# Who adds and who multiplies: moving GpSimd's share in the scan stages of a decoder layer

## What is computed

```
def step(h, inputs):
    d_t, B_t, C_t, u_t = inputs
    dA = jnp.exp(d_t[..., None] * A)
    h = h * dA + (d_t * u_t)[..., None] * B_t[:, None, :]
    y = jnp.einsum('bdn,bn->bd', h, C_t)
    return (h, y)
...
y = jnp.swapaxes(ys, 0, 1) + u * D
y = y * jax.nn.silu(jnp.transpose(z, (0, 2, 1)))
return jnp.einsum('md,bld->blm', out_proj_weight, y)
```

## Time and profile before

| | |
|---|---|
| median of 3 runs | 1690.67 us (1690.46 to 1693.57) |
| the profiled execution | 1690.69 us, its span 1688.9 us |
| PE busy | 1438.1 us, 85% |
| DVE busy | 1341.3 us, 79% |
| POOL busy | 1059.8 us, 63% |
| ACT busy | 798.7 us, 47% |
| chain that ended last | PE 55%, DVE 17%, issue 12%, ACT 8%, POOL 7% |

### The profile page before, as it was taken

The page is one execution under the profiler, slowest core; times in us unless marked ns, Lnnn a source line. Parts: engine busy times, 40 slices in busy tenths (PEclk is TensorE's granted clock), DMA queues, the critical chain, the costliest instruction groups (busy, mean ns, idle before and its releaser), DMA issues.

```text
span 1688.9 us, 19487 instructions
## 1 busy us (share of the span) xinstructions
PE 1438.1 (85%) x5448; PEld 834.8 (49%) x5456; DVE 1341.3 (79%) x2215; ACT 798.7 (47%) x1370; POOL 1059.8 (63%) x684
## 2 busy tenths in 40 slices
PE   7587669999699899999699899999699999737994
PEld 4333224444565565444465565444465665326783
DVE  3588999676799999786899999796899999784212
ACT  3676444246634565246634565246634565231141
POOL 0299899102999899402999899401999999422101
PEclk9889899999699999999699999999699999967997
DMA  3550000413535673613535674612534773600984
GB/s 114 224 187 25 1 0 23 146 32 109 198 137 182 205 236 126 212 38 105 227 118 188 208 235 138 212 38 101 231 113 163 226 235 124 249 25 20 349 331 142
DMA packets 94074, 252.14 MB, mean 149 GB/s; under 512 B 11024, under 2 KB 11152, under 8 KB 88848
## 3 DMA queue, kind: packets, MB, share of 16 engines
q1 hardware_dynamic: 86688, 229.93, 40.1%
q0 software_dynamic: 5120, 16.78, 3.1%
q10 hardware_dynamic: 2160, 4.19, 0.6%
HBM read 207.87 MB, written 42.99 MB: 149 GB/s over the span
## 4 chain that ended last, share of the span: by engine, by line
PE 55%; DVE 17%; issue 12%; ACT 8%; POOL 7%; DMA 1%; DVEq 0%; POOLq 0%; SPq 0%; ACTq 0%
PE bank L1936 11%; PE bank L1796 7%; DVE bank L1269 5%; PE bank L2062 5%; PE bank L1809 5%; PE bank L1868 4%; PE bank L1873 4%; POOL work L662 3%; PE bank L1965 3%; PE bank L1957 3%; PE bank L1862 3%; DVE work L1281 2%; PE bank L1912 2%; DVE pairs L1281 2%; PE bank L1837 2%
## 5 line engine op out<-in xcount | busy, mean ns | idle before, releaser
L662 POOL TENSOR_TENSOR work<-du,BB 128x1024 f32<-128x1024 f32 x255 | 598.7, 2357 | 5.2 <-DVE work L1545 4.4
L941 ACT ACTIVATE bank<-delta,A_sb 128x512 f32<-128x512 f32 x512 | 350.0, 690 | 471.9 <-DVE pairs L1281 257.8
L1269 DVE TENSOR_TENSOR_SCAN bank<-bank,work 128x512 f32<-128x512 f32 x432 | 522.6, 1219 | 7.8 <-POOL work L662 4.0
L1936 PEld LDWEIGHTS bank<-x3T,ew_up 128*128 128x128 f32 x1488 | 220.7, 196 | 74.3 <-issue 63.2
L1936 PE MATMUL bank<-x3T,ew_up 128*128 128x128 f32 (+1 forms) x1488 | 242.8, 310 | 5.2 <-issue 5.2
L1281 DVE TENSOR_TENSOR pairs<-bank,CB 128x512 f32<-128x512 f32 x240 | 161.6, 673 | 3.9 <-PE bank L1873 2.9
L607 POOL TENSOR_TENSOR col<-col,halfpow 128x4 f32<-128x4 f32 (+1 forms) x8 | 7.8, 973 | 208.1 <-DVE col L1421 208.1
L1281 DVE TENSOR_TENSOR work<-bank,CB 128x512 f32<-128x512 f32 x192 | 128.7, 670 | 0.0
L1809 PE MATMUL bank<-xT,wst 128*128 128x512 f32 x256 | 120.2, 616 | 9.1 <-DVE ew_up L1258 7.0
L1868 PE MATMUL bank<-pairs,ident 128*128 128x512 f32 x160 | 87.5, 630 | 41.8 <-POOL pairs L717 16.7
L2062 PE MATMUL bank<-wst,zg 128*128 128x512 f32 x256 | 117.0, 593 | 0.9 <-DVE zg L1289 0.9
(11 more groups left out here) (256 smaller groups left out, 2511.8 us busy)
## 6 DMA issues: line engine op xcount, KB each, us to landing
ew_up<-in_exp_w SPq DMA_DIRECT2D x93, 512.0 KB, 3.7
ew_dn<-in_exp_w SPq DMA_DIRECT2D x93, 256.0 KB, 4.3
hm<-xs_dram SPq DMA_DIRECT2D x69, 256.0 KB, 4.6
ys_dram<-x3T SPq DMA_DIRECT2D x69, 256.0 KB, 4.6
wst<-in_w_in SPq DMA_DIRECT2D x64, 256.0 KB, 2.7
BB<-bc_dram SPq DMA_DIRECT2D x16, 1024.0 KB, 7.4
CB<-bc_dram SPq DMA_DIRECT2D x16, 1024.0 KB, 9.4
wst<-in_out_w SPq DMA_DIRECT2D x32, 256.0 KB, 2.9
```

What stands on the lines that cost most here:

```text
L662: nc.gpsimd.tensor_tensor(dBu[:, k % CHUNK_SLOTS, :, :], du[:, j % 2:j % 2 + 1, :].broadcast_to([P, 2, T]), BB[:, n0:n0 + 2, :], ALU.mult) ...
L941: nc.scalar.activation(R[q % RING][:, :], delta[:, j, :], ACT.Exp, scale=A_sb[:, j, n:n + 1]).then_inc(S["da_ready"], 1)
L1269: V.tensor_tensor_scan(prod[c % (2 * PAIR_SLOTS)] if on_pool(q) else R[q % RING][:, :], R[q % RING][:, :], dBu[:, c // 2 % CHUNK_SLOTS, c ...
L1936: ins = mm(gu_bank(v)[:, part * n:(part + 1) * n], w[:, part * D + k * P:part * D + (k + 1) * P], rhs, start=(k == 0), stop=(k == KD - 1))
```

## The change

Two rules change, with all that counts by them. `on_pool` is now true for every fourth unit (3, 7, 11, ...) in all batches; in batch 0 it was so already. POOL sums pairs 0, 4, 8, ... instead of 0, 2, 4, ....

```
 def on_pool(q):
-    return q % 8 in ((3, 7) if q < UNITS else (7,))
+    return q % 4 == 3

 def pool_pairs(m):
-    return (max(m - PAIRS, 0) + 1) // 2
+    return (max(m - PAIRS, 0) + 3) // 4

 (POOL, pair(m))
-                    if m % 2 == 0 and b > 0:
+                    if m % 4 == 0 and b > 0:
                         pool.wait_ge(S["prod_done"], dve_products(UNITS * b + 2 * m + 2))
                         nc.gpsimd.tensor_tensor(lo, lo, hi, ALU.add).then_inc(S["pair_ready"], 1)
                     elif on_pool(UNITS * b + 2 * m + 1):

 (PE, nsum(m))
-                    if m % 2 == 0 and b > 0:
+                    if m % 4 == 0 and b > 0:
                         pe.wait_ge(S["pair_ready"], pool_pairs(PAIRS * b + m + 1))
                         mm(Y[:, :], ident[:], prod[2 * (m % PAIR_SLOTS)], start=(m % (NS // 2) == 0),
                            stop=False).then_inc(S["nsum_done"], 1)
```

## The result

| | before | changed |
|---|---|---|
| median | 1692.11 us (1690.46 to 1693.57, 4 runs) | 1708.97 us (1705.57 to 1709.88, 4 runs) |
| ratio | | 1.0096, 95% interval 1.0075 to 1.0117: 16 us slower by the ratio |
| profiled execution, span | 1690.69, 1688.9 us | 1709.88, 1708.2 us |

A second timing of the changed kernel, beside later experiments, gave 1.0095 (1.0071 to 1.0119). The forecast was 1693.2 us, with a range to 1702: too low. One execution of `e14_middle_gate_later` took 3899 us, and the median of that run is given without it.

What follows compares the result with a forecast made beforehand. No single bound: PE, DVE and POOL all nearly full, with PE ending the stage in batches 1 and 2. Terms of +0.6, +1.7 and +0.2 for batches 1 to 3 gave +2.5 on 1690.69, so 1693.2 us; range 1684.5 to 1702.

Steps and rivals of the forecast that it cites:

- PE's idle is not absorbed: Rival: half of PE's waits stay despite the added matmuls, 14.2 us on top of the sum, 1707.4 us; chance 0.14.
- (b): Positions 34 to 56 of a stage: DVE gains one product, PE's idle takes the added matmuls; −0.6 us a batch.
- (a): Stage start to the first routed rows, position 34: the token rows' load sets the end, so 0; bounds −0.6 and +1.
- (c): Positions 56 to 72, statistics and catch-up: +0.3 us, with the clock drop going, −1.8 in batch 2, −2.9 in batch 1.
- The term of the clock: Catch-up behind the statistics: added matmuls fill PE's wait and the clock drop goes, −2.9 us in batch 1, −1.8 in batch 2.
- (d): Positions 72 to 110: five added matmuls into little PE idle, +1.2 us in batches 1 and 2, +0.4 in batch 3.
- (e): Output projection, position 110 to the end: three matmuls on a full PE, +2.6 us in batches 1 and 2.
- the cover that I named: Behind batch 3's stage: 3.6 us of slack before DVE reads PE's transposes cover PE's 2.6 us.
- POOL was not late: Rival, POOL becomes late: PE waits for its products, +3.8 us on top of the sum, 1697.0 us; chance 0.06.
- DVE's saving came through: Faster rival: nearly all PE idle at positions 34 to 110 goes, −5.1 us, 1685.6 us; chance 0.22.

Runs made afterwards that it cites:

- e14_middle_gate_later: Kernel before with the change only in pairs 20 to 51 of batches 1 to 3 and DVE's gate at 6 there: 1680.69 us, 0.9927.
- e10: Changed kernel, gate at 5, with the old rule for pairs 0 to 19 of batches 1 to 3: 1699.5 us, 1.0058 to the kernel before.
- e6: Changed kernel with DVE's gate at 6 instead of 5 in batches 1 to 3 only: 1691.3 us, 1.0004 to the kernel before.
- e2: Kernel before with only the products moved to POOL, which still sums every second pair: 1705.49 us, 1.0075.
- e3: Changed kernel with PE leaving out one product of every pair 2 (mod 4), so the old number of matmuls: 1685.66 us, 0.9965 to the kernel before.
- e1: Changed kernel with the products taken back to DVE, only the sums of the change kept: 1714.32 us, 1.0133 to the kernel before.
- e4: Changed kernel with DVE's gate at 6 instead of 5 in all batches: 1691.68 us, 1.0008 to the kernel before.
- e7: Changed kernel with DVE's gate at 7 in batches 1 to 3: 1689.59 us, 0.9996 to the kernel before.
- e11: Changed kernel with the products taken back to DVE and the gate at 6 in batches 1 to 3: 1698.37 us, 1.0056 to the kernel before.
- e5: Kernel before with DVE's gate one position later, at 6, in batches 1 to 3 only: 1679.86 us, 0.9938.

## Why the prediction was wrong

**What bounds the kernel.** That PE ends a stage, that three engines are near full and that PE would become the bound were right. Among the rivals, "PE's idle is not absorbed", at 1707.4 us, is the one that came, with 0.14. Its condition was met: 6.0 of PE's 10.2 us of waits in batch 2 stayed, and L1965's stayed at 3.2, not below 2. That its sum came so near is in part luck, since it prices waits that are not filled, and half of the surplus arose in (b), from matmuls that met no wait.

**Step (a) and (b), the step that failed.** I had written that POOL and the load of the token rows set the point at p = 34, "so this point stays: 0", and of the next stretch that PE's idle is "enough for the two or three matmuls". The load did stay: it is issued 901.90 − 823.35 = 78.6 us after the stage's start in the changed kernel, 896.47 − 817.81 = 78.7 before. But PE no longer waits for it. The stretch ahead of it and the first transposes of token rows (L1912) before the change:

```profile
860.00:892.00 32.00, 32.00 (x107) 20.14 (x106) 31.77 (x45) 12.37 (x21) 30.67 (x21) 1.00 0.44 156
...
899.29 0.66 PE L1912 MATMUL bank<-ident,hm 128*128 128x128 f32 x4 [0.22 <-DMA hm<-xs_dram]
```

and the load and the transposes after it:

```profile
901.90 0.80 SPq L460 DMA_DIRECT2D hm<-xs_dram  x2
...
906.48 0.60 PE L1912 MATMUL bank<-ident,hm 128*128 128x128 f32 x4
```

The transposes start 906.48 − 823.35 = 83.1 us into the stage instead of 899.29 − 817.81 = 81.5. Three matmuls (pairs 6, 10, 14), 2.6 us, fell into visits where PE had no idle time at all. PE came to them 0.6 us earlier than before, and the wait for the rows took in 0.4, not the 0.7 that I had set against them: those 0.7 us of waiting at L1936 stand behind the rows, at 87.6 us of the stage, and are still there at 89.2. I took the room of PE from windows behind this stretch and gave none of my rows to the stretch itself. From there PE comes late to each gate and DVE is held, 3.05 and 1.78 us in (b), more than its saved products are worth. Instead of −0.6 a batch, (b) was +1.7 to +1.9; e10, which undoes the pairs before 20, gives at least 6 us back.

**Step (c).** The term of the clock was the second. I let the drop go in both batches, −1.8 and −2.9. In batch 2 it stayed (0.90 against 0.89), in batch 1 it shrank (0.90 against 0.83). PE's longest wait before it, 2.1 us at L1965, was not filled, for it is a wait for ACT's copy (L1002), which comes behind a decay on ACT that waits for a product of DVE:

```profile
961.38 0.69 ACT L941 ACTIVATE bank<-delta,A_sb 128x512 f32<-128x512 f32 x1 [1.28 <-DVE work L1281]
...
962.17 0.58 ACT L1002 COPY x3T<-bank 128x512 f32<-128x512 f32 x1
...
962.89 1.51 PE L1965 MATMUL bank<-ew_dn,etm 128*128 128x512 f32 x2 [2.10 <-ACT x3T L1002]
```

In e6, where little of PE's waiting is left, the granted clock in the same stretch is 1.00:

```profile
952.00:968.00 16.00, 16.00 (x82) 10.72 (x82) 16.00 (x25) 11.38 (x21) 16.00 (x10) 1.00 0.77 214
```

By the rule of the Trainium skill (TensorE: Matmul & The Clock Gate, Part 1) idle time throttles the engine; e6 agrees, and so does the changed kernel, whose longest idle time stayed. But the idle time of such a stretch does not settle whether the drop comes. In e10 batches 1 and 2 have the same stretch, with the same wait of 2.1 us at its end, and only batch 1 has the drop behind it (in each pair of lines, the stretch and what follows):

```profile
555.20:572.20 17.00, 14.79 (x72) 9.48 (x72) 16.92 (x31) 8.80 (x18) 11.94 (x8) 1.00 0.67 213
572.20:589.00 16.80, 16.65 (x77) 11.23 (x78) 13.83 (x22) 9.16 (x18) 16.80 (x10) 0.90 0.62 189
...
941.40:958.40 17.00, 14.79 (x72) 9.48 (x72) 16.92 (x31) 8.73 (x17) 11.98 (x8) 1.00 0.68 212
958.40:975.00 16.60, 16.57 (x83) 11.13 (x84) 15.12 (x24) 10.24 (x18) 16.60 (x10) 1.00 0.66 200
```

Positions 56 to 72 take 33.9 us in the one and 32.3 in the other, so a drop is worth 1.6 us; what decides it stays open. What failed was my step from more matmuls to less idle time, and the drop was never as certain as the sum had it.

**Step (d)** was right in batch 2 (+1.3, forecast +1.2). In batch 3 it was +1.2, not +0.4.

**Step (e)** had the right mechanism and was somewhat small: 2.6 forecast, 3.4 and 4.2 measured in batches 2 and 1. In batch 2 it adds up as in (b): 2.2 us more at one gate and 0.9 at the last, 1.5 more before the last scan, less two products. Batch 1's further 0.8 stand beside a granted clock of 0.72 at 726 to 732 us, which was 1.00 at the same place of batch 2. In batch 3 the cover that I named exists: DVE's last scan came 5.4 us later in its stage, 1.7 of them in (e) where I had taken about 0, and the batch ended 3.6 later.

**The sum.** −0.6 → +1.7 or more in (b) is 7 us over three batches, the clock and the rest of (c) 4, (d) and (e) 3: 14 on top of the forecast's 2.5.

**The rivals.** POOL was not late: in the whole of batch 2's stage PE waits once for one of its products in the changed kernel, 1.2 us at 23.6 us of the stage, and (a) is no longer for it. POOL is late when it gets 16 operations more (e2). A product on DVE still takes 671 ns. DVE's saving came through to 6 us (e3) where PE's load was the old one.

## What to carry to other kernels

When engines are all near full, price an added instruction stretch by stretch, by the idle time of its engine in that very stretch: here the 24 exchanges in the middle of the stages cost 3 to 5 us and the 24 at their ends 11 to 13. Where one engine waits for another at fixed places of its program, ask how late the other may be; one number that lets it be a unit later was worth 10 us on the kernel before and 17 on the changed one, which it brought back to the time of the kernel before. Idle time of an engine that itself waits for a late result of another is not filled by giving it more work: PE's wait at L1965 was 2.1 us before and after.

## What the runs showed beyond that

An engine's saved work can come back as waiting: from e1 to the changed kernel DVE loses 16 products a batch, 9.4 us, PE's matmuls stay as they are, and the waits at the gate in batch 2's stage rise from 12.0 to 18.2 us, two thirds of the saving. The other 6.6 us of the rise, from 5.4 to 12.0, come with PE's matmuls alone. And the clock's drop behind the statistics is not fixed to the kernel. In the changed kernel PE was busy 14.86 us of the 17 before the drop, and the granted clock of the next 17 us was 0.90, a short time at 1.2 GHz among 2.4. No such drop stands in batches 1 and 2 of e4, e6, e7, e11 and e14, with the gate at 6 or 7, nor in e2, with the gate at 5, but in e5, whose gate is at 6, it is there in both (0.90 and 0.89). With e10 beside it, a drop of this kind is better priced at a chance than as lost or won.
